# A decoder of eight layers on one core: seams between stages woven together, later weights made in five parts, Fourier attention issued step by step

## The reference, cut to what matters

```python
x = x + L0_attn(norm(x))   # moving average over time, a matmul, and a convolution of 5 taps
x = x + L0_ffn(norm(x))    # 16 experts of width 64, the 4 best of each token weighted by a router
x = x + L1_attn(norm(x))   # attention in windows of 64 tokens, 16 heads of 8
x = x + L1_ffn(norm(x))    # 16 experts and a shared one, the 2 best
x = x + L2_attn(norm(x))   # gated scan over time
x = x + L2_ffn(norm(x))    # 8 experts of width 256, the 2 best
x = x + L3_attn(norm(x))   # Fourier attention with its own MLP of 512
x = x + L3_ffn(norm(x))    # MLP of 512
```

```python
p  = einsum('blhd,dm->blhm', x, proj_mat) / sqrt(8)         # 8 -> 128 phases
qp = concatenate([cos(p), sin(p)]) / sqrt(128)              # from q; kp the same from k
kv = einsum('blhm,blhd->bhmd', kp, v)                       # sums over all tokens
attn = einsum('blhm,bhmd->blhd', qp, kv)
```

## Time and profile before

| what | us |
|---|---|
| median of 3 runs | 853.26 |
| lowest and highest | 849.58, 856.47 |
| the profiled execution | 855.7 |
| its span, first to last instruction | 853.9 |
| start of the first experts' first block | 47.8 |
| start of the first attention's projection of its last chunk | 294.0 |
| first cosine and end of the last sine of the Fourier stage | 562.8, 783.4 |

### The profile page before, as it was taken

How to read it: one execution, slowest core, us unless ns; L and a number is a source line. 1 busy time by engine, 2 the same in 40 slices (tenths; PEclk the granted TensorE clock), 3 DMA queues, 4 the chain that set the end, 5 groups by cost and what they waited for, 6 DMA issues and landing times.

```text
span 853.9 us, 11872 instructions
## 1 busy us (share of the span) xinstructions
PE 699.8 (82%) x3850; PEld 463.0 (54%) x3850; DVE 628.9 (74%) x1469; ACT 560.4 (66%) x861; POOL 376.1 (44%) x389
## 2 busy tenths in 40 slices
PE   4887999888887799999689999967677677676787
PEld 3666778555554477877467677722222222222665
DVE  6676786765665467787667889988788788786784
ACT  5253667747665356655546668758699899787575
POOL 6628665431331135454259977823322234411330
PEclk9889999958796679999869999989899999899999
DMA  4200000100100000000000000000000000000001
GB/s 139 74 12 15 16 16 13 41 26 13 38 20 13 1 2 1 1 1 1 0 14 25 0 1 1 2 0 1 0 1 1 0 1 1 0 1 0 2 1 50
DMA packets 9613, 11.65 MB, mean 14 GB/s; under 512 B 720, under 2 KB 5712, under 8 KB 9552
## 3 DMA queue, kind: packets, MB, share of 16 engines
q1 hardware_dynamic: 9552, 10.89, 4.5%
HBM read 9.84 MB, written 1.05 MB: 13 GB/s over the span
## 4 chain that ended last, share of the span: by engine, by line
PE 43%; DVE 18%; ACT 16%; POOL 13%; issue 9%; DMA 0%; DVEq 0%; ACTq 0%; POOLq 0%
POOL rbuf L1048 3%; PE y_bank L740 3%; PE up_banks L1334 3%; PE gate_banks L740 2%; PE gate_banks L742 2%; PE gate_banks L741 2%; DVE B L1824 2%; PE y_bank L742 2%; PE y_bank L741 2%; POOL WL L2247 2%; PE up_banks L740 2%; ACT B L1837 2%; PE up_banks L742 2%; PE up_banks L741 2%; ACT B L1834 2%
## 5 line engine op out<-in xcount | busy, mean ns | idle before, releaser
L1048 POOL TENSOR_TENSOR rbuf<-B,rbuf 128x512 fp32r<-128x512 f32 x96 | 124.3, 1296 | 85.0 <-ACT rbuf L971 84.6
L1007 DVE TENSOR_TENSOR B<-B,up_banks 128x512 f32<-128x512 f32 x68 | 46.5, 684 | 47.9 <-PE up_banks L742 25.4
L956 ACT ACTIVATE B<-gate_banks 128x512 f32<-128x512 f32 x68 | 40.6, 598 | 60.9 <-PE gate_banks L742 59.7
L1023 DVE TENSOR_TENSOR B<-B,spread_bank 128x512 f32<-128x512 f32 x96 | 64.7, 679 | 10.5 <-PE spread_bank L906 4.7
L971 ACT ACTIVATE rbuf<-B 128x512 fp32r<-128x512 f32 x100 | 62.5, 625 | 13.8 <-DVE B L1023 10.9
L740 PE MATMUL gate_banks<-XH,WH 128*128 128x512 f32 x152 | 67.6, 445 | 0.8 <-ACT YT L1416 0.8
L1834 ACT ACTIVATE B<-B,VEC 128x1024 f32<-128x1024 f32 x48 | 55.4, 1155 | 14.2 <-DVE B L1829 14.2
L742 PE MATMUL gate_banks<-XH,WL 128*128 128x512 f32 x152 | 63.2, 416 | 0.0
L741 PE MATMUL gate_banks<-XL,WH 128*128 128x512 f32 x152 | 63.1, 415 | 0.0
L960 ACT ACTIVATE B<-gate_banks,WR 128x512 f32<-128x512 f32 x64 | 43.8, 686 | 21.4 <-PE gate_banks L742 20.7
L503 POOL TENSOR_SCALAR small<-small 128x4 f32<-128x4 f32 x32 | 8.5, 264 | 110.2 <-DVE small L393 109.6
(11 more groups left out here) (353 smaller groups left out, 2154.2 us busy)
## 6 DMA issues: line engine op xcount, KB each, us to landing
STG<-in_w_split SPq DMA_DIRECT2D x27, 256.0 KB, 2.7
X<-in_x SPq DMA_DIRECT2D x4, 256.0 KB, 4.9
out<-X SPq DMA_DIRECT2D x4, 256.0 KB, 2.3
WR<-in_w_raw SPq DMA_DIRECT2D x1, 524.5 KB, 4.4
STG<-in_w_exact SPq DMA_DIRECT2D x2, 256.0 KB, 2.8
STG<-in_w_split SPq DMA_DIRECT2D x5, 64.0 KB, 1.9
STG<-in_w_split SPq DMA_DIRECT2D x1, 192.0 KB, 2.3
STG<-in_w_split SPq DMA_DIRECT2D x1, 128.0 KB, 2.1
```

Source lines behind the costliest of these rows:

```text
L1007: nc.vector.tensor_tensor(MO[n % 2], AO[n % 2], U[n % 2][:, :], ALU.mult).then_inc(mul_done, 1)
L1023: nc.vector.tensor_tensor(hidden(f, n), src, spread_bank(f, c, b), ALU.mult).then_inc(h_ready, 1)
L1048: e_.tensor_tensor(lo, hidden(f, n), hi.bitcast(F32), ALU.subtract).then_inc(hl_ready, 1)
```

## The change

It moves instructions on four engines and adds almost none.

1. **First stage.** TensorE no longer puts the transposes of the first experts' norm ahead of the last chunk's tap matmuls, but after 9 of their 15 (`front_pe(pe, 1, 0, 2)` at k == 3), and the router matmuls only after that chunk; the transposes of the next norm stand behind the experts' first two blocks. ScalarE loads the exponential's table with a tiny activation before the last `YT`. VectorE's low part of chunk 3's state goes ahead of the split of that norm. GpSimd splits its last piece behind the first norm's small steps.
2. **Later weights** are made in five parts, at (chunk, block) (1, 1), (1, 4), (2, 1), (2, 4) and (3, 1) of the first experts.
3. **Attention to second experts.** The four matmul groups of the second experts' first two blocks are placed among the last turns and ahead of the projection; the Silu table is loaded and block 0 activated before the projection's copy.
4. **Third experts to Fourier stage.** The phases of pair 0 are made behind the down matmuls of the last chunk's block 12, rounded on VectorE before the last `YT`; the sine table is loaded before that `YT`; the clearing of `KVT` goes from VectorE to GpSimd; the four buffers of a pair are numbered anew.
5. **Fourier stage.** TensorE makes the phases one pair at a time, ahead of each use, and the projection right behind them; ScalarE takes the projection's copy one pair earlier. In the queries the norm's steps move to earlier pairs on three engines.

```diff
@@ first stage @@
             for k in range(TAPS):
                 if c == NC - 1 and k == 3:
-                    hook(4)
+                    front_pe(pe, 1, 0, 2)
...
         def stage0_act(a, chain, c, hook):
             if c == NC - 1:
-                hook(4)
+                nc.scalar.activation(first_table, zero, ACT.Exp)
...
+        def late_turn(n, c, pos):
+            return pos == 2 and (n, c) in ((1, 0), (1, 1))
...
                 if late_start(f, c, b):
                     up(c, 1)
+                    if f is FFN0:
+                        front_pe(pe, 1, 1, 2)
                     hook(LATE_ROUTE)
@@ later weights: later_weights is split into four functions @@
+        LATER_AT = {(1, 1): 0, (1, 4): 1, (2, 1): 2, (2, 4): 3, (3, 1): 4}
...
         def ffn_pool(g, chain, f, c, hook, work):
-            if f is FFN0 and c == 1:
-                later_weights(g, chain)
             for b in range(f.blocks):
+                part = LATER_AT.get((c, b), -1) if f is FFN0 else -1
+                if part == 0:
+                    head_weights(g, chain)
+                if part == 1:
+                    phase_products(g, chain)
+                if part in (2, 3):
+                    phase_parts(g, chain, part - 2)
+                if part == 4:
+                    clear_values(g, chain)
@@ attention, last chunk, TensorE @@
                 weigh(NU - 1)
+                ffn_weights(pe, FFN1)
+                pe.wait_ge(xl_ready, count(FFN1.norm, 0) + 1)
+                pe.wait_ge(pt_ready, NU - 1)
+                ffn_second(pe, FFN1, 0, 0)
                 pe.wait_ge(o_read, NU - 2)
                 attn_turn_out(pe, NU - 2)
                 attn_turn_out(pe, NU - 1)
+                pe.wait_ge(pt_ready, NU)
+                ffn_second(pe, FFN1, 0, 1)
                 attn_turn_pe(pe, c)
                 hook(10)
+                pe.wait_ge(o_read, NU)
+                ffn_first(pe, FFN1, 0, 0)
+                ffn_first(pe, FFN1, 0, 1)
                 attn_project_pe(pe, c)
@@ third experts, last chunk @@
+                    if f is FFN2 and at_ == (NC - 1, f.blocks - 4):
+                        pe.wait_ge(phase_weights, 1)
+                        pe.wait_ge(act_done, f.block0 + NC * f.blocks)
+                        lin_phases(pe, 0)
...
+                if f is FFN2:
+                    nc.scalar.activation(junk[:, 0:1], zero, ACT.Sin)
                 result(c)
...
                     for k in (2, 1):
                         low(nc.vector, v, f, block_no(f, c, f.blocks - k))
+                    if f is FFN2:
+                        lin_round_dve(v, 0)
+                        lin_rest(v, 0)
+                        lin_abs(v, 0)
@@ Fourier stage @@
-        RA = [B[:, 4 * k_:4 * k_ + 4, :].rearrange("p a b -> p (a b)") for k_ in range(3)] + [S0[:, :]]
+        RA = [S0[:, :]] + [B[:, 4 * k_:4 * k_ + 4, :].rearrange("p a b -> p (a b)") for k_ in range(3)]
...
         def lin_pool(g, cp, hook):
             if cp == 0:
                 body_start(g, 6, 0)
+                nc.gpsimd.memset(KVT[:, :, :, :].rearrange("p s j m -> p (s j m)"), 0.0).then_inc(kvt_cleared, 1)
...
-                lin_hooks(n, hook, 1, {0: (0,), 1: (1,)} if cp < NC else {2: (0,), 3: (1,)})
+                lin_hooks(n, hook, 1, {0: (0,), 1: (1,)})
...
         def lin_pe(pe, cp, hook):
...
-                if n % 2 == 0:
-                    lin_phases(pe, p + 2)
-                    lin_phases(pe, p + 3)
+                lin_phases(pe, p + 2)
+                if lin_projects(cp + 1, n) is not None:
+                    lin_proj_pe(pe, cp + 1, lin_projects(cp + 1, n))
...
                 lin_use(pe, p)
-                if lin_projects(cp + 1, n) is not None:
-                    lin_proj_pe(pe, cp + 1, lin_projects(cp + 1, n))
...
-                    lin_hooks(n, hook, 5, {4: (2,)})
+                    lin_hooks(n, hook, 5, {3: (2,)})
         def lin_act(a, cp, hook):
...
                 lin_cos(a, p)
-                if lin_projects(cp + 1, n - 1) is not None:
-                    lin_proj_act(a, cp + 1, lin_projects(cp + 1, n - 1))
+                if lin_projects(cp + 1, n) is not None:
+                    lin_proj_act(a, cp + 1, lin_projects(cp + 1, n))
...
-                lin_hooks(n, hook, 3, {3: (2,)} if cp < NC else {5: (2,)})
+                lin_hooks(n, hook, 3, {3: (2,)} if cp < NC else {4: (2,)})
         def lin_dve(v, chain, cp, hook):
...
-                    lin_hooks(n, hook, 2 if cp == 0 else 4, {0: (0,), 1: (1,), 2: (11,), 4: (3,)})
+                    lin_hooks(n, hook, 2 if cp == 0 else 4, {0: (0,), 1: (1,), 2: (11,), 6: (3,)})
                 else:
-                    lin_hooks(n, hook, 7, {1: (0,), 3: (1,), 6: (3,)})
+                    lin_hooks(n, hook, 7, {0: (0,), 2: (1,), 6: (3,)})
```

138 lines of the change are left out of this document (87 added, 51 removed).

## The result

The changed kernel takes 827.9 us (median of four runs, 825.9 to 832.5) against 853.8 (849.6 to 856.5), a ratio of 0.968, 95% interval 0.964 to 0.973. The forecast was 822, range 810 to 838. A second set of six runs of the changed kernel gave 829.9 (825.7 to 837.6). One run of all that follow, of turn1 at 840.3, lies more than 1.5% above the fastest of its kernel, counts as slow and stays out of its median. The profiled execution took 827.8 us with a span of 826.0, so 27.9 less than the profiled one of before, where the forecast had 31.3.

A forecast was written before the change was run, and what follows sets the result against it. No engine is full (TensorE busy 82%), so only waiting can be gained. Five places sum to -31.3 us from the profiled 855.7, giving 824.4, or 822 for the median; range 810 to 838.

The forecast's parts named there:

- the likeliest case: Whole kernel: the forecast itself, all five places gaining as estimated, 822 us for the median; chance 0.58.
- A, first stage: First stage: nine tap matmuls move into TensorE's wait for XN, so routing comes earlier; -4.0 us, bounds 4.5 and 1.5.
- B, later weights: First experts: GpSimd's work in five parts mostly fits between blocks; 5.4 - 1.3 - 0.8, taken as -3.3 us.
- C, the seam: Attention into second experts: two blocks and a wait move ahead of the projection; -5.0 us, bounds 6.5 and 3.0.
- D, start of the stage: Third experts to Fourier stage: pair 0 ready early, so the first cosine comes sooner; -2.6 us, bounds 2.8 and 1.5.
- The rule's price of up to 0.9: Start of Fourier stage: GpSimd's clearing could block VectorE's abs of pair 0, returning up to 0.9 us, time 823.
- E, the loop: Fourier loop's eight chunks: phases one pair at a time, earlier projection and norm steps; -16.4 us, bounds -25.3 and -8.
- The floor of a chunk is then the busier of ScalarE and VectorE: Fourier chunks after the change: length falls to the busier engine's time plus a remainder of 0.64 us.
- So the projection comes late: Fourier loop before: phases queue ahead of the projection, so ScalarE's copy waits (2.23 us at 608.63) and VectorE in turn.
- Half of the loop: Fourier loop: bursts of norm steps on VectorE, not order, lengthen chunks 1, 2, 7; loop -8.2, 830 us; chance 0.22.
- Slower: the clock: Fourier chunks 3 to 6: more frequent TensorE pauses lower the granted clock; +15, 868 us; chance 0.03.
- signs of being wrong: Fourier stage: chunks 1, 2, 7 over 30 us, clock under 0.9 in chunks 3 to 6, WK copies waiting over 2.

The follow-up runs named there:

- turn1: Changed kernel, but in the first chunk of queries alone phases, projections and their copies ordered as before; median 835.9 us (three runs).
- u_ends: Changed kernel with the first stage and the start of the Fourier stage as before; median 837.7 us (two runs).
- later2: Changed kernel with two of the five later-weights parts moved, to block 3 of chunks 2 and 3; median 827.0 us (two runs).
- u_order: Changed kernel with only the Fourier loop's order as before, the norm's steps at their new places; median 830.4 us (two runs).

## Why the prediction was right, and where it was not

The range held the time, and the likeliest case, with 822, missed by 5.9. Its parts fared differently, and 3.8 us of the profiled gain were none of them.

- **A, first stage.** -4.0; the runs show 3.3 to 5.4. The sum was right and the path only in part. The router matmuls came just 2.0 earlier (39.18 for 41.16), for nine matmuls of the last chunk still stand between the transposes and them. What the filled wait moved is the end of that chunk, and VectorE's first step on the router's result stands behind the residual addition that needs it: that step went from 45.83 to 40.70. u_ends takes all moves of the first stage back at once, so what each is worth is not shown.
- **B, later weights.** The gain of 5.4 in chunk 1 was right, and so was the slack at (2, 1): from the gate's activation to YT it is 3.08 (97.62 to 100.70) where it was 1.70 (107.86 to 109.56), so YT is 1.4 late, and 1.3 was forecast. The term that failed is what the part at (2, 1) costs besides: nothing was put for VectorE, whose XN took 4.21 beside GpSimd's unbroken work instead of 1.38. TensorE's transposes wait 0.93 more for it, and the next gate is 2.5 late; the stretch lost 3.0. In later2, with that part moved, XN is back at 1.38 and the gate in time. It is the same effect that D names and that E leaves out.
- **C, the seam.** -5.0; measured 7.4, above the bound of 6.5. The mechanism was right and the size off: everything was priced at the low level (0.425 a matmul, and before the change the stretch had a clock of 0.66), and after the change the rest of the seam mostly ran at a higher one. Where it did not, in u_order at 0.59, the gain is 5.2, near the forecast's own figure.
- **D, start of the stage.** -2.6; measured 2.4. The cover held: ScalarE's round of pair 1 hides abs, even with the 0.25 that the clearing on GpSimd cost it. The rule of the Trainium skill ("SBUF — State Buffer", section "Who interferes with whom") is borne out by these traces: of the 15 abs in the changed kernel that took longer than 0.75 us, each ended 0.54 to 0.56 after the end of a GpSimd instruction that ran when it was issued. Not every recorded overlap counts: the abs at 545.20 began beside GpSimd's small step of 128x4, recorded from 544.43 for 1.50, and took its 0.69. The rule's price of up to 0.9 at this place did not come.
- **E, the loop: -16.4, measured -10.0.** This is where the forecast missed most. "The floor of a chunk is then the busier of ScalarE and VectorE" held in chunks 1, 3, 4 and 7 (forecast -3.3, -1.3, -1.2, -5.7; measured -3.0, -0.6, -1.5, -5.6). Chunk 2 was to lose 5.4 and lost 2.3: the floor was taken from VectorE's old busy time, 24.84, and it is now 26.93. Three of the chunk's abs began beside GpSimd's splits and are 1.9 us longer together, where before one was, by 0.1. The floor's rise is 2.1 of the 3.1 missed; of VectorE's idle time, 2.5, one wait for ScalarE's round is 1.9. How the loss splits between chunks 1 and 2 differs from one execution to the next; together they were forecast at 55.6 and took 59.0 to 60.2 in six profiles. Over the stage the stretched abs take 6.9 us more than 0.69 each, where they took 2.6, and XN in chunk 7 took 3.94 where it had been 2.35:

```profile
593.18 1.29 POOL L1820 TENSOR_TENSOR WL<-WK,WL 64x512 fp32r<-64x512 f32 x1
...
593.49 1.53 DVE L1912 TENSOR_SCALAR B<-B 128x1024 uint32<-128x1024 uint32 x1
...
710.82 3.94 DVE L413 TENSOR_SCALAR XN<-Z,small 128x128 f32<-128x128 f32 x4
```

  Chunk 5 was to grow by 1.0 and grew by 4.1. The forecast had named the cause, phases and projection behind the use that waits for KVT, and gave it too small a price: the wait before the second copy is 6.43, and the first one delays the sums that KVT is made of. turn1, with the old order in this chunk alone, takes the 4.1 back (27.19). Of the growth of chunks 5 and 6 together, 5.7, it takes back 3.4; for the rest u_order points at the norm's new places.
- **What explains the long chunks.** "So the projection comes late", with VectorE waiting in turn, was given as the reason for chunks 1 and 2, and the projection's copy was said to wait over 2 us "in most pairs with a projection". The trace of before doesn't bear this out: of the 28 copies of the stage four wait over 1 us, three of them in chunks 1 and 2 (2.1 to 2.4) and one at the turn, while in chunk 2 VectorE waits 3.64 in one piece for the copy of the turned norm, ahead of its split. The runs say so too: with the old order and the new places of the norm's steps these two chunks are as short as in the changed kernel (29.1 and 29.5, or 58.7 together). In the keys only one place differs, VectorE's split of the norm, two pairs later, and that wait is gone. That the projection's wait cost something is true of chunks 3 and 4 alone, 2.1 us together.
- **Not forecast: the clock of attention, -3.8.** This was the luck of the two profiled executions. It made up for much of E's shortfall; without it the profiled difference would be 24 and not 28, still inside the range.
- **The rivals.** "Half of the loop" came nearest: -10.0 against its -8.2, and its reason, bursts of norm steps on VectorE, is what u_order shows. "Slower: the clock" did not come: the middle chunks stayed between 0.93 and 1.00, but for the chunk with the turn, at 0.84, where TensorE had waited 2.70 for the copied sums and 1.06 for KVT. Two of the forecast's own signs of being wrong stand in that chunk, a clock under 0.9 and a copy to WK that waits over 2 us (6.43). XN without its 4.01 and the matmuls of 53.60 earlier (47.67) are signs that held; the first cosine came 2.59 after YT, where under 2.5 was asked.

The 1.7 us that the changed kernel's profile loses behind the Fourier stage are no part of the change: from the end of the last sine the profiles of this one code take 70.2 to 72.3, and the kernel before took 70.5. Open: which of the other steps of the norm (TensorE, ScalarE or VectorE) makes the rest of chunk 7, and which makes chunks 5 and 6 longer.

## What to carry to other kernels

When an engine works through a fixed list, look at what stands behind each wait rather than at the wait: two small GpSimd steps of 1.2 us behind three splits cost 3.8 us, and a loop order that does no harm in the other chunks cost 4 in the one that holds a long wait, where it should have stayed as it was. A floor taken from busy time moves when work is packed closer on engines that block each other. And read a change by the stretches that it touches, over several profiles: the Fourier stage repeated to 1%, its single chunks to some 2 us, while one median of three runs came out 8 us on the wrong side of a gain of 3.
